# The first stage of a one-core transformer layer: coefficients on GpSimd, normalisation sums on ScalarE

## The reference, cut to what matters

```python
dt = exp(log_dt); A = -exp(inv_A_real) + 1j * A_imag          # H = 128 channels, N = 64 states
dtA = A * dt
Cc = B * C * (exp(dtA) - 1.0) / A                             # C: 16 batches x 128 channels x 64 states
V = exp(dtA[:, :, None] * arange(1024))
h = 2.0 * einsum('chn,hnl->chl', Cc, V).real                  # 16 x 128 x 1024
h = h + attention(layernorm(h))
h = h + ffn(layernorm(h))
```

## Time and profile before

| | |
|---|---|
| time, median of 3 | 2041.17 us (2038.68 to 2045.85) |
| profiled execution: time, span | 2039.54 us, 2037.7 us |
| TensorE busy | 1884.0 us, 92% of the span |
| VectorE, ScalarE, GpSimd busy | 1163.9, 615.4, 614.3 us |
| first stage: barrier behind it | about 236.6 us |
| granted TensorE clock, whole span | 0.987 |

### The profile page before, as it was taken

One profiled execution on the slowest core, in us unless ns is written; L12 is line 12 of the kernel. 1 busy time (PEld: TensorE's weight loads), 2 busy tenths in 40 slices (PEclk: granted clock), 3 DMA queues, 4 the chain that ended last, 5 costly groups with the idle time before them and its releaser, 6 DMA issues.

```text
span 2037.7 us, 31325 instructions
## 1 busy us (share of the span) xinstructions
PE 1884.0 (92%) x13212; PEld 1023.7 (50%) x13212; DVE 1163.9 (57%) x1476; ACT 615.4 (30%) x871; POOL 614.3 (30%) x261
## 2 busy tenths in 40 slices
PE   0377699999999999999999999999999999999999
PEld 0367566656666665545554444444444444444444
DVE  8999568777787878756644544444444445111011
ACT  2055333433433444421113333333333333200000
POOL 2676023433434333533112222223223222101101
PEclk9998699999999999999999999999999999999999
DMA  2022211111021222144433223223223222543341
GB/s 92 11 62 62 56 42 56 33 46 34 19 82 58 79 56 79 63 162 148 162 104 115 87 69 104 81 75 104 78 78 102 75 83 79 194 145 114 128 145 42
DMA packets 99812, 173.32 MB, mean 85 GB/s; under 512 B 13984, under 2 KB 75168, under 8 KB 91744
## 3 DMA queue, kind: packets, MB, share of 16 engines
q1 hardware_dynamic: 99680, 171.41, 26.2%
HBM read 114.22 MB, written 56.11 MB: 84 GB/s over the span
## 4 chain that ended last, share of the span: by engine, by line
PE 76%; DVE 7%; POOL 2%; issue 1%; ACT 1%; DMA 0%; ACTq 0%; DVEq 0%
PE acc L1140 15%; PE acc L1214 15%; PE acc L1141 15%; PE ps_p L944 3%; PE ps_p L946 3%; PE ps_p L945 3%; PE acc L1058 3%; PE acc L1060 2%; PE acc L1059 2%; PE ps_t L971 2%; PE ps_p L960 2%; PE ps_p L962 2%; PE ps_p L961 2%; PE ps_l L1156 2%; POOL prob L904 1%
## 5 line engine op out<-in xcount | busy, mean ns | idle before, releaser
L1140 PE MATMUL acc<-x_hi,q_f 128*128 128x512 f16 x1376 | 522.0, 379 | 0.0
L1141 PE MATMUL acc<-x_lo,q_f 128*128 128x512 f16 x1376 | 521.5, 379 | 0.0
L1214 PE MATMUL acc<-down_levels,hid_parts 128*128 128x512 f16 x1376 | 300.1, 379 | 0.0
L904 POOL TENSOR_TENSOR prob<-prob,mx 128x1024 f32<-128x1024 f32 x64 | 121.4, 1898 | 383.7 <-DVE mx L1497 383.7
L1140 PEld LDWEIGHTS acc<-x_hi,q_f 128*128 128x128 f16 x1376 | 134.6, 98 | 174.8 <-issue 17.8
L1214 PEld LDWEIGHTS acc<-down_levels,hid_parts 128*128 128x128 f16 x1376 | 133.2, 98 | 163.1 <-issue 5.0
L1141 PEld LDWEIGHTS acc<-x_lo,q_f 128*128 128x128 f16 x1376 | 134.7, 98 | 156.9
L915 POOL TENSOR_SCALAR q_f<-q_raw 128x2048 f16<-128x2048 int32 x22 | 118.0, 5366 | 314.1 <-PE acc L1141 312.5
L944 PE MATMUL ps_p<-x_hi,w_qk 128*128 128x512 f16 x512 | 194.7, 380 | 0.0
L945 PE MATMUL ps_p<-x_lo,w_qk 128*128 128x512 f16 x512 | 194.0, 379 | 0.0
L946 PE MATMUL ps_p<-x_hi,w_qk 128*128 128x512 f16 x512 | 194.0, 379 | 0.0
(11 more groups left out here) (285 smaller groups left out, 3072.5 us busy)
## 6 DMA issues: line engine op xcount, KB each, us to landing
q_raw<-in_gu_q SPq DMA_DIRECT2D x22, 1024.0 KB, 7.3
hidden_parts<-hidden SPq DMA_DIRECT2D x42, 512.0 KB, 3.5
hid_parts<-hidden_parts SPq DMA_DIRECT2D x15, 1376.0 KB, 6.5
down_raw<-in_down_q SPq DMA_DIRECT2D x22, 512.0 KB, 5.2
w_raw<-in_w_qk SPq DMA_DIRECT2D x8, 1024.0 KB, 4.9
h_tokens<-n_tok SPq DMA_DIRECT2D x16, 512.0 KB, 3.8
o_parts<-ot SPq DMA_DIRECT2D x32, 256.0 KB, 2.3
wv_raw<-in_w_o SPq DMA_DIRECT2D x8, 1024.0 KB, 5.1
```

The lines of the kernel that those rows point to most:

```text
L904: nc.gpsimd.tensor_tensor(prob[s % 2][p][:], prob[s % 2][p][:], bc(mx[p][:], H, 2), ALU.subtract).then_inc(s_sub[p], 1)
L1140: nc.tensor.matmul(acc[u % 2][:, m, :], lev, x2_hi[:, k, tok], start=(k == 0), stop=False)
L1141: last = nc.tensor.matmul(acc[u % 2][:, m, :], lev, x2_lo[:, k, tok], start=False, stop=(k == KT - 1))
L1214: last = nc.tensor.matmul(acc[n % 2][:, b, :], parts[n % 3][:, at], levels[:, i, b * CH:(b + 1) * CH], start=(i == 0 and part == 0), stop= ...
```

## The change

The front: GpSimd does the chain of the coefficients (series, quotient, `a` and `b`), as instructions of 128 or 256 elements, and neither of its two 4096-wide products. ScalarE makes the magnitudes by 32 exponentials of 128 elements, each with its step as scale. VectorE makes the phases in two halves of 64 channels with PSUM as their room, folds by clearing the sign bit, multiplies both tables, and computes 2/|A|² itself; ScalarE takes 2 x 7 sines. The second half's tables and rotations are done by VectorE between units 0 to 3.

The loop: its Python loops are unrolled over the 16 units. The product is issued in two halves of four channels, each with its PSUM buffer and its copy; `v_second` lies in PSUM. ScalarE accumulates the sum of a tile as it copies it, VectorE scales that to minus the mean, ScalarE squares the tile with this as bias and accumulates again, and takes the root. `find_tops` moves to the front, `find_big` to step 6, the exchange behind the eighth store, `find_scale` to step 11, and the weight split to step 15. Orders per step: see the loops below. In `find_big` two maxima become one instruction.

The diff, cut to its core (whole renamed waits and unchanged arithmetic are left out):

```diff
-        v_second = mag_room[:, 2, :]
...
-        stats = [sb(f"n_stats{s}", [P, 2, 6]) for s in two]
-        mv = [sb(f"n_mv{s}", [P, 2]) for s in two]
-        std = [sb(f"n_std{s}", [P, 1]) for s in two]
+        total, square, minus_mean, std = ([sb(f"n_{n}{s}", [P, 1]) for s in two] for n in ("total", "square", "mean", "std"))
...
+        with ExitStack() as tables_only:
+            phase_ps = [tables_only.enter_context(nc.psum_tensor(f"phase_ps{k}", [P, HALF_H, TAB], F32)) for k in two]
+        ps = [st.enter_context(nc.psum_tensor(f"ssm_ps{s}", [P, UH // 2, P], F32)) for s in two]
+        v_second = st.enter_context(nc.psum_tensor("v_second", [P, UH * P], F32))
...
-            with sp.Fori(0, VIS) as n:
-                for s in two:
-                    sp.wait_ge(s_tok[s], n + 2)
-                    sp.dma_start(h0_dram[:, channels(n, s), :], tok[s][:]).then_inc(s_out[s], 16)
-            first.exchange(sp, 0)
+            for u in range(UNITS):
+                sp.wait_ge(s_tok, u + 1)
+                sp.dma_start(h0_dram[:, channels(u), :], tok[u % 2][:]).then_inc(s_out[u % 2], 16)
+                if u == UNITS - 9:
+                    first.exchange(sp, 0)
...
-            pool.wait_ge(s_z, 1)
-            nc.gpsimd.tensor_tensor(mag[:], bc(t[2][:], TAB, 2), bc(steps[:], H, 1), ALU.mult).then_inc(s_decay, 1)
...
-            nc.gpsimd.tensor_tensor(tab2, tab2, mag[:], ALU.mult).then_inc(s_tab2, 1)
...
+            pool.wait_ge(s_im, 1)
+            y, y2, sin, cos = t[6], t[8], series[:, 0, :], series[:, 1, :]
+            chain.after(ts(y2[:], t[3][:], MAGIC, None, ALU.add))
+            chain.after(ts(y2[:], y2[:], MAGIC, None, ALU.subtract))
+            chain.after(tt(y[:], t[3][:], y2[:], ALU.subtract))
...
+            chain.after(tt(series[:], bc(y2[:], 2, 1), bc(taylor[:, 5, :], H, 2), ALU.mult))
+            for k in range(4, -1, -1):
+                chain.after(tt(series[:], series[:], bc(taylor[:, k, :], H, 2), ALU.add))
+                chain.after(tt(series[:], series[:], bc(y2[:], 2, 1), ALU.mult))
+            chain.after(ts(series[:], series[:], 1.0, None, ALU.add))
+            chain.after(tt(sin, sin, y[:], ALU.mult))
+            chain.mark(tt(y[:], sin, cos, ALU.mult))
+            chain.after(tt(t[7][:], sin, sin, ALU.mult))
...
+            a, b = t[7], t[8]
+            pool.wait_ge(s_square, 1)
+            chain.after(ts(t[10][N:P, :], t[6][N:P, :], -1.0, None, ALU.mult))
+            for dst, rows, of in ((a, slice(0, N), t[6]), (a, slice(N, P), t[9]), (b, slice(0, N), t[9]), (b, slice(N, P), t[10])):
+                tt(dst[rows, :], of[rows, :], inverse_square[rows, :], ALU.mult).then_inc(s_ab, 1)
+            pool.wait_ge(s_ab, 4)
...
+                if u >= 2:
+                    pool.wait_ge(s_mm, 2 * (u - 1))
+                nc.gpsimd.tensor_tensor(four(v[s], TJ), bc(tab1[:, ch, TI:2 * TI], TJ, 3), bc(tab1[:, ch, 2 * TI:TAB], TI, 2),
...
+            for k in range(UNITS + 2):
+                if each(0, k):
+                    product(k, 0)
+                if each(1, k):
+                    to_tokens(k - 1)
+                if each(0, k):
+                    product(k, 1)
+                if each(2, k):
+                    to_features(k - 2)
...
-            act.wait_ge(s_decay, 1)
...
-            nc.scalar.activation(mag[:], mag[:], ACT.Exp).then_inc(s_mag, 1)
...
+            for k, step in enumerate(STEPS_OF):
+                last = nc.scalar.activation(mag[:, :, k], t[2][:], ACT.Exp, scale=float(step))
+            last.then_inc(s_mag, 1)
...
+                nc.scalar.activation(tok[u % 2][:].rearrange("p (i j) -> p i j", j=P), pt[:], ACT.Identity,
+                                     accum_out=total[u % 2][:]).then_inc(s_tok, 1)
+            def squares(u):
+                act.wait_ge(s_mean, u + 1)
+                act.wait_ge(s_tab, 2)
+                if u >= 2:
+                    act.wait_ge(s_trn, u - 1)
+                nc.scalar.activation(nrm[u % 2], tok[u % 2][:], ACT.Square, bias=minus_mean[u % 2][:],
+                                     accum_out=square[u % 2][:]).then_inc(s_sq, 1)
+            def deviation(u):
+                act.wait_ge(s_sq, u + 1)
+                nc.scalar.activation(std[u % 2][:], square[u % 2][:], ACT.Sqrt, scale=1.0 / D, bias=eps[:]).then_inc(s_std, 1)
...
+            for k in range(UNITS + 3):
+                if each(3, k):
+                    high(k - 3)
+                if each(2, k):
+                    normalise(k - 2)
+                if each(0, k):
+                    columns(k, 0)
+                if each(1, k):
+                    tokens(k - 1)
+                if each(0, k):
+                    columns(k, 1)
+                if each(1, k):
+                    squares(k - 1)
+                    deviation(k - 1)
+                if k == UNITS - 1:
+                    act.wait_ge(s_v, UNITS)
+                    for part in two:
+                        first.high(nc, act, 0, part)
...
+            def phases(k):
+                hs, turn = heads(k), phase_ps[k]
+                chain.after(tt(turn[:], bc(t[3][:, hs], TAB, 2), bc(steps[:], HALF_H, 1), ALU.mult))
+                chain.after(ts(tab1[:, hs, :], turn[:], MAGIC, MAGIC, ALU.add, ALU.subtract))
+                chain.after(tt(turn[:], turn[:], tab1[:, hs, :], ALU.subtract))
+                chain.mark(ts(tab1[:, hs, pair].bitcast(I32), turn[:, :, pair].bitcast(I32), 0x7FFFFFFF, None, ALU.bitwise_and))
+                chain.mark(ts(tab1[0:N, hs, j0].bitcast(I32), turn[0:N, :, j0].bitcast(I32), 0x7FFFFFFF, None, ALU.bitwise_and))
+                ts(tab2[N:P, hs, j0].bitcast(I32), turn[N:P, :, j0].bitcast(I32), 0x7FFFFFFF, None, ALU.bitwise_and).then_inc(s_phase, 1)
+            phases(0)
+            chain.mark(tt(inverse_square[:], t[1][:], t[1][:], ALU.mult))
+            chain.after(tt(nrm0[:, 0:H], aim, aim, ALU.mult))
+            chain.after(tt(inverse_square[:], inverse_square[:], nrm0[:, 0:H], ALU.add))
+            chain.after(nc.vector.reciprocal(inverse_square[:], inverse_square[:]))
+            ts(inverse_square[:], inverse_square[:], 2.0, None, ALU.mult).then_inc(s_square, 1)
+            phases(1)
...
+            def tables(k):
+                hs = heads(k)
+                dve.wait_ge(s_trig, k + 1)
+                chain.mark(tt(tab1[:, hs, :], tab1[:, hs, :], mag[:, hs, :], ALU.mult))
+                tt(tab2[:, hs, :], tab2[:, hs, :], mag[:, hs, :], ALU.mult).then_inc(s_tab, 1)
...
+            dve.wait_ge(s_mag, 1)
+            tables(0)
+            dve.wait_ge(s_tab, 1)
+            for part in range(3):
+                rotations(0, part)
+            first.find_tops(nc, dve, chain)
...
-            def moments(n, s):
-                dve.wait_ge(s_tok[s], n + 2)
-                chain.mark(nc.vector.bn_stats(stats[s][:, 0, :], tok[s][:, 0:512]))
-                chain.mark(nc.vector.bn_stats(stats[s][:, 1, :], tok[s][:, 512:D]))
-                apart(dve, s_passed, (s_dve, chain.now()))
-                nc.vector.bn_aggr(mv[s][:], stats[s][:].rearrange("p a b -> p (a b)")).then_inc(s_mv[s], 1)
...
+            def mean(u):
+                dve.wait_ge(s_tok, u + 1)
+                if u >= 2:
+                    dve.wait_ge(s_rs, u - 1)
+                ts(minus_mean[u % 2][:], total[u % 2][:], -1.0 / D, None, ALU.mult).then_inc(s_mean, 1)
+            def inverse(u):
+                dve.wait_ge(s_std, u + 1)
+                if u >= 2:
+                    dve.wait_ge(s_nrm, u - 1)
+                chain.after(nc.vector.reciprocal(rs[u % 2][:, 0:1], std[u % 2][:]))
+                tt(rs[u % 2][:, 1:2], minus_mean[u % 2][:], rs[u % 2][:, 0:1], ALU.mult).then_inc(s_rs, 1)
...
+            for k in range(-1, UNITS + 3):
+                if each(-1, k):
+                    second_factor(k + 1)
+                if each(2, k):
+                    inverse(k - 2)
+                if each(-1, k):
+                    second_power(k + 1)
+                    power(k + 1)
+                if each(3, k):
+                    low(k - 3)
+                if k == 0:
+                    tables(1)
+                    dve.wait_ge(s_tab, 2)
+                if 1 <= k < 4:
+                    rotations(1, k - 1)
+                if k == UNITS - 10:
                     first.find_big(nc, dve, chain, 0)
-                if n == 1:
+                if k == UNITS - 5:
                     first.find_scale(nc, dve, chain, 0)
-            run(dve, [(4, inverse), (0, factors), (3, moments), (5, low)], chain, 2 * 4, weights)
-            first.low(nc, dve, 0, 0)
-            first.low(nc, dve, 0, 1)
+                if each(1, k):
+                    mean(k - 1)
+                if k == UNITS - 1:
+                    for part in two:
+                        first.low(nc, dve, 0, part)
...
-        chain.after(nc.vector.tensor_tensor(self.big_v[:], self.big_v[:], self.top[:, 2, 2 * g:2 * g + 1], ALU.max))
```

(61 more changed lines are left out.)

303 lines of the change are left out of this document (118 added, 185 removed).

## The result

The changed kernel takes 2004.62 us (median of 4, 2003.63 to 2006.01) against 2040.62 for the kernel before: ratio 0.982, 95% interval 0.9801 to 0.984, so 36 us less. The prediction said 1999 us, range 1983 to 2022.

The account below looks back on a forecast made before the run. The first stage, 0 to 236.6 us, delays all behind its barrier one for one. Front 54.9, loop 111 and tail 28.7 sum to 194.6, 42 us less: span 1995.7, execution 1997.5, forecast 1999 us, range 1983 to 2022.

Parts of the forecast that it names:

- Front: First stage up to the first unit's factors: these at 54.9 us in place of 75.4, a gain of 20.5.
- the first call's 6 us: GpSimd's coefficient chain: skill page's cost of about 6 us for newly loaded code; the prediction gave it nothing.
- Loop: First to sixteenth unit's factors: 15 x 6.8 + 9 = 111 us against 118.8, a gain of 7.8.
- Tail: Last unit's factors to the barrier: about 28.7 us against 42.4, a gain of 13.7.
- Dear GpSimd instructions: Rival, front's coefficient chain: small GpSimd instructions at 0.83 us each, rotations(0) 13.3 us later, 2012 us; chance 0.12.
- a floor of 1.5 us: Slower case, GpSimd's chain: about 1.5 us an instruction loses the gain; at 2 us each 2064 us; chance 0.025.
- Table reloads: Rival, ScalarE in the loop: Square and Sqrt share no table, two loads of 1.28 per unit, 2023 us; chance 0.015.
- TensorE's bound: Rival, loop: TensorE becomes the bound at a period of 5.9 us, 13.5 us earlier, 1986 us; chance 0.06.
- The period kept: Rival, loop: stages still wait in turn, TensorE clocks down, period 7.9 us, 16.5 us later, 2016 us; chance 0.17.
- the sign that I had set: Loop: the prediction is wrong if the period stays above 7.5 us; a unit every 6.8 us was expected.
- The sum: Whole stage: 54.9 + 111 + 28.7 = 194.6 us in place of 236.6, 42 us less, giving 1999 us.
- one SBUF operand does not: VectorE beside GpSimd: two SBUF operands on VectorE and a GpSimd instruction exclude each other, one does not; no size given.

Follow-up runs that it names:

- Experiment 12: Changed kernel with find_tops, find_big and tables(1) ahead of the first rotation, exchange ahead of the stores, mean ahead of rotations(1) and find_scale: 1994.76 us, ratio 0.9769.
- Experiment 4: Changed kernel with find_tops and find_big between tables(0) and the first rotations, and the exchange ahead of the stores: 1998.31 us, ratio 0.9794.
- Experiment 5: Kernel before, with only find_tops and find_big moved ahead of its loop and the exchange ahead of its stores: 2042.01 us, ratio 1.0009.
- experiment 8: Changed kernel with find_big early, VectorE's reciprocal and shift behind the next unit's powers, ScalarE's normalise behind the second columns: 2009.15 us, ratio 0.9842.

## Why the prediction was right, point by point

*Front: right in its sum, 54.9 forecast and 54.97 measured.* Part of that is luck. The whole stage runs 1.15 us earlier than I had it: the first parameter load is issued at 3.82 and not 4.97, and I had costed the diff's effect ahead of it at nothing. The diff drops the eighteen increments of semaphores that SP did there; the load is issued at 3.67 to 4.06 in all twelve profiled kernels with the change and at 4.97 and 4.80 in the two without, but no run drops the increments alone. The chain takes 33.3 us where I said 35.6: 0.45 and 0.53 for 0.47 and 0.5, 0.61 to 0.72 for 0.6 to 0.8, and 8.4 us behind VectorE's products for 9.6. Against this stand 3.4 us of waits behind the chain: the first rotation 2.44 for 0.69, beside GpSimd's next product, and the bias tops 1.78 for 0.15. The rounding from PSUM takes 2.29 for 2048, as much as one of 4096 took in SBUF. This agrees with the Trainium skill's "VectorE: DVE Perf Modes", "Why PSUM operands drop a tier", by which an fp32 operand in PSUM leaves one element a cycle. tables(0) starts at 37.3 for 39.6, and as forecast nothing hangs on when it does. Of the first call's 6 us, cited in the prediction, nothing is seen: the first instruction's 2.54 end 0.39 us behind VectorE's product, and the three other long ones end 0.32 to 0.70 us behind theirs.

*Loop: the step that failed, 116.8 for 111.* Both of its terms were off, in opposite ways. An undisturbed unit takes 6.2, not 6.8. The disturbances cost 116.8 - 15 x 6.2 = 23.8 us, not 9. By unit: tables(1) and rotations(1) 12.9 over the four units behind the first (I said 7), find_big 7.4 over three (3.9 + 1.1 + 2.3; I said 2 with find_scale), find_scale 2.2, the rest 1.3. I priced inserted work by its own length less VectorE's slack. But it stands in line ahead of mean(u - 1), and a late mean is paid again by ScalarE's queue and by TensorE's. Experiment 12 shows this for the rotations, by moving the mean alone: 4.9 us. Experiment 4 shows that find_big's 4.0 us cost 7.8 of the loop (109.0 for 116.8) and 6.3 of the time; it takes the work away with the delay, so that for find_big the way over the mean rests on the lines above. It is not the whole: with find_big and tables(1) in the front and the mean ahead, experiment 12's units three to seven are still 9.8 us above five of 6.2, and why is open. Nor did a run test what sets the 6.2.

*Tail: 29.6 for 28.7.* The terms that I wrote there add up to 28.2, so half a microsecond of the forecast has no term. The exchange leaves at 136.88, find_scale starts at 155.46 without a wait. Experiment 5 bears on the size: in the kernel before, find_big and the exchange out of the tail shorten it by 8.0 of the 12.7.

*Rivals.* Dear GpSimd instructions and a floor of 1.5 us fall by the 0.45 and 0.53 above. Table reloads fall: behind the one ACT_TABLE_LOAD at 81.36, for the first root, none stands in the stage. TensorE's bound: not reached, but an undisturbed unit of 6.2 is near it; the last stretch above has TensorE busy 5.35, VectorE 4.81, GpSimd 6.00 (its waits for VectorE counted in) and ScalarE 6.03 of it, so the sums have left ScalarE as full as any. The period kept: its mean is 7.8 with the inserted work, close to the 7.9 of before, and for the reason that I gave it, stages that wait in turn and a colder TensorE. The mean also crosses the sign that I had set, a period above 7.5; but my own forecast, inserted work included, was a mean of 7.4, and the undisturbed unit is well below, so the sign was badly put. The rival's price, 16.5 us above my loop, didn't come: the loop is 5.8 above it.

*The sum.* -20.5 - 2.0 - 12.7 - 0.7 behind the barrier = -35.9 us of span for my -42. The loop's 5.8 and the tail's 1.0 are that difference, less the 0.7 behind the barrier that I hadn't forecast. That so large an error in the inserted work shows so little is luck as well: the shorter unit gave 9 of its 14.8 us back.

## What to carry to other kernels

Where several engines work a unit in turn by hand-written orders, price inserted work by what stands behind it in its queue, not by its length: put short instructions that others wait for ahead of it, and long work where its engine is idle. When a queue is reordered, add up the ring that the new order closes before trusting the wait that it removes: opening 0.8 us of VectorE's idle time cost 7 to 11 us of the whole here. With ScalarE's order altered too, or alone, a ring of 7.35 us over ScalarE and TensorE took the place of units of 6.2. And a wait that looks dear in a steady period may not set it; change that wait alone and see if the period moves.

## What the runs showed of the hardware

- An fp32 instruction of GpSimd and one of VectorE with both operands in SBUF held each other up, either way, down to the smallest: 128x128 on GpSimd took 2.5 for 0.45 behind a VectorE product, and a VectorE product of one element 1.88 for 0.16 beside GpSimd's.
- My reading "one SBUF operand does not" in the prediction rested on an instruction with the other operand in PSUM, and holds for only some with a single SBUF source: a VectorE *tensor_scalar* of 16 elements took 1.78 for about 0.16 beside GpSimd's (53.08). The one of one element took its 0.15 in the midst of a GpSimd instruction (98.01), and find_big's reduction of 2048 its 2.27 (117.06). What parts these no run shows.
- The one that begins first, be it by 0.02 us, keeps its own time: the power at 112.21 in experiment 4 took 1.22 and GpSimd's product, begun at 112.23, 2.98 for 1.92. In experiment 8 GpSimd's began at 116.33, and the power at 116.94 took 2.96.
- A GpSimd instruction of 128x128 costs 0.40 (one operand) to 0.53 us, with a wait on itself 0.08 more; the same on VectorE 0.28 and 0.23.
